# Which states' B-row multiplies VectorE takes in a token scan: state 12 in place of state 4

## The reference

```python
def scan_step(h, inputs):
    x_t, dt_t, B_t, C_t = inputs
    A_bar = jnp.exp(dt_t[..., None] * A)
    B_bar = dt_t[..., None] * B_t[:, None, :]
    h_new = A_bar * h + B_bar * x_t[..., None]
    y_t = (h_new * C_t[:, None, :]).sum(axis=-1)
    return (h_new, y_t)
```

## Time and profile before

| what | value |
|---|---|
| median of 3 runs | 335.23 us (334.68 to 344.01) |
| the profiled execution's own time | 334.67 us |
| its span | 332.9 us |
| busy, TensorE | 274.3 us (82%) |
| busy, VectorE | 264.8 us (80%) |
| busy, GpSimd | 256.7 us (77%) |
| busy, ScalarE | 191.6 us (58%) |

### The profile page before, as it was taken

How to read it: one execution, slowest core, us unless ns; L and a number is a source line. 1 busy time by engine, 2 the same in 40 slices (tenths; PEclk the granted TensorE clock), 3 DMA queues, 4 the chain that set the end, 5 groups by cost and what they waited for, 6 DMA issues and landing times. The chain is left out here.

```text
span 332.9 us, 4726 instructions
## 1 busy us (share of the span) xinstructions
PE 274.3 (82%) x1454; PEld 156.9 (47%) x1454; DVE 264.8 (80%) x289; ACT 191.6 (58%) x300; POOL 256.7 (77%) x134
## 2 busy tenths in 40 slices
PE   7899918875778589999889789997695787997996
PEld 4423402333435244346564243464564656765674
DVE  3465687998768898998798989998898887999711
ACT  2103931326895433478967354689738686888253
POOL 0009037999999998998999989999998689999500
PEclk9999976999798879999999899999969799999999
DMA  7980297587779999767699997676999999998301
GB/s 234 410 318 0 50 335 293 185 261 248 254 269 265 316 295 398 257 239 278 209 318 289 321 345 269 232 248 228 312 275 318 344 275 342 324 340 297 97 0 32
DMA packets 46889, 85.88 MB, mean 258 GB/s; under 512 B 7697, under 2 KB 24593, under 8 KB 46609
## 3 DMA queue, kind: packets, MB, share of 16 engines
q1 hardware_dynamic: 46464, 84.42, 76.5%
q10 hardware_dynamic: 400, 1.17, 1.3%
HBM read 75.62 MB, written 1.57 MB: 232 GB/s over the span
## 5 line engine op out<-in xcount | busy, mean ns | idle before, releaser
L1254 POOL TENSOR_TENSOR hc<-h,c_row 128x1024 f32<-128x1024 f32 (+1 forms) x79 | 154.4, 1963 | 16.9 <-DVE h L1383 13.8
L1243 POOL TENSOR_TENSOR ub<-u,b_row 128x1024 f32<-128x1024 f32 (+1 forms) x47 | 95.6, 2034 | 15.7 <-DMA b_row<-bc_dram 14.9
L951 ACT ACTIVATE decay<-delta,neg_a 128x512 f32<-128x512 f32 (+1 forms) x62 | 49.9, 815 | 65.4 <-DVE h L1383 65.2
L684 PEld LDWEIGHTS acc_y<-pack,hc 128*128 128x128 f32 x512 | 61.3, 149 | 47.9 <-issue 27.5
L684 PE MATMUL acc_y<-pack,hc 128*128 128x128 f32 x512 | 75.7, 289 | 9.9 <-POOL hc L1254 6.2
L1383 DVE TENSOR_TENSOR_SCAN h<-decay,ub 128x512 f32<-128x512 f32 (+1 forms) x40 | 64.9, 1621 | 15.4 <-POOL ub L1243 10.7
L626 PE MATMUL work<-q,kT 64*128 64x512 f32 x112 | 34.9, 702 | 17.8 <-DVE mixed L1409 13.5
L1409 DVE TENSOR_TENSOR mixed<-gam,work 128x512 f32<-128x512 f32 x56 | 35.6, 676 | 7.3 <-PE work L626 6.6
L978 ACT ACTIVATE decay<-u 128x512 f32<-128x512 f32 (+1 forms) x44 | 27.8, 639 | 20.7 <-DVE h L1383 20.4
L637 PE MATMUL acc_r<-mixed,v_sb 128*64 128x512 f32 x128 | 37.0, 658 | 1.1 <-DVE mixed L1409 1.0
L1383 DVE TENSOR_TENSOR_SCAN h<-decay_own,decay 128x512 f32<-128x512 f32 (+1 forms) x24 | 35.7, 1487 | 1.2
(11 more groups left out here) (226 smaller groups left out, 353.4 us busy)
## 6 DMA issues: line engine op xcount, KB each, us to landing
b_row<-bc_dram SPq DMA_DIRECT2D x64, 512.0 KB, 5.3
c_row<-bc_dram SPq DMA_DIRECT2D x64, 512.0 KB, 5.4
group_w<-expert_w SPq DMA_DIRECT2D x48, 128.0 KB, 4.7
gam<-gammaT SPq DMA_DIRECT2D x8, 512.0 KB, 10.4
expert_w<-routed_w SPq DMA_DIRECT2D x1, 2048.0 KB, 18.4
gam<-expert_w SPq DMA_DIRECT2D x16, 128.0 KB, 5.2
x_in<-xT SPq DMA_DIRECT2D x4, 256.0 KB, 9.2
pack<-packed ACTq DMA_DIRECT2D x1, 788.0 KB, 7.4
```

The source lines that it names most:

```text
L684: mm = nc.tensor.matmul(acc_y[:, to:to + P], hc[:, at:at + P], ident, start=(job.state == 0 and c % 4 == 0), stop=(job.state == STATES - 1 ...
L951: op = nc.scalar.activation(target, delta[:, job.image % 2, columns], ACT.Exp, scale=neg_a[:, job.state:job.state + 1])
L1243: nc.gpsimd.tensor_tensor(ub[:, ring(made, job.halves)], u[:, job.image % 2, tokens(q)], b_row[:, ring(job.at, job.halves)], ALU.mult).the ...
L1254: nc.gpsimd.tensor_tensor(hc[:, here], h[:, here], c_row[:, here], ALU.mult).then_inc(hc_ready, job.halves)
```

## The change

In images one to three VectorE drives states 0, 8, 10, 12 and 14, where it drove 0, 4, 8, 10 and 14. The last image is as before.

```diff
 VECTOR_JOBS = [q for q, job in enumerate(JOBS)
-               if job.state in ((0, 4, 8, 10, 14) if job.image not in SPLIT else (0, 2, 4, 5, 7, 9, 11, 13, 15))]
+               if job.state in ((0, 8, 10, 12, 14) if job.image not in SPLIT else (0, 2, 4, 5, 7, 9, 11, 13, 15))]
```

## The result

The changed kernel takes 345.92 us (median of 4 runs, 344.30 to 348.12), the kernel before 334.96; the ratio is 1.034, with a 95% interval of 1.029 to 1.039. The direction was right and the size was not: 341.7 us was forecast, with a range up to 344. The profiled execution of the changed kernel took 348.12 us (span 346.3), the longest of its four: 13.4 us over the span of 332.9 before, where the median shows 11.

What follows compares the result with a forecast made beforehand. GpSimd and VectorE, both nearly full, were taken to bound the kernel together, neither alone. Delays of 2.35, 3.15 and 1.55 us in images one to three make 7.05, taking 334.67 to 341.7 us; range 339.5 to 344.

Steps and rivals of the forecast that it cites:

- GpSimd's row without a pause: First half of images one to three: GpSimd's unbroken states 1 to 7 delay state 7's scan, 2.9 us in all.
- the waits of s5 to s7 for ub: Sign, first half: scans of states 5, 6 and 7 would each wait for GpSimd's ub; no size given.
- ScalarE's decay_own in front of V12: Second half: ScalarE's extra decay delays VectorE's state 12 multiply; 1.75 us each in images two and three.
- V12 waits: Sign at state 12: VectorE's multiply would wait about 1.6 us for ScalarE's copy.
- In image one 0.65 was forecast: Second half, image one: state 13's scan 0.65 us late, since an existing 0.80 us wait for GpSimd goes.
- TensorE's order is unchanged and the W that it waits for come with the scans.: TensorE, images one to three: its queue keeps its order and its W inputs follow the scans; costed at nothing.
- Of what follows in VectorE's queue nothing has waited, so the delay stays.: VectorE behind state 12, image two: following work had no waits to absorb the 1.75 us delay.
- State 14 is late as well: Rival: state 14's copy also comes late in each image, adding 5.2 us, 346.9 us; chance 0.06.
- The last image: Sign: the last image's length, from its first scan on, would be unchanged.
- By occupancy nothing changes.: Whole kernel: equal busy sums and GpSimd's same occupancy would leave 334.7 us; rival's chance 0.07.

Runs made afterwards that it cites:

- e1: Half the change against the kernel before: state 4 goes to GpSimd, state 12 stays there; 340.92 us, ratio 1.013.
- e9: The changed kernel itself, run again beside the kernel before on another chip; 346.53 us, ratio 1.039.
- e10: The changed kernel plus spare matmuls in TensorE's pauses in all three images; 342.56 us, ratio 1.026.
- e11: Control: the kernel before plus nine spare matmuls on TensorE in image two; 335.25 us, ratio 1.0035.
- e2: Other half alone against the kernel before: VectorE drives state 12 as well as 0, 4, 8, 10, 14; 343.55 us, ratio 1.029.
- e4: The change made in image two alone, images one and three as in the kernel before; 341.60 us, ratio 1.023.
- e5: The changed kernel with ScalarE's softplus parts moved behind the two copies of u for state 12; 341.71 us, ratio 1.020.
- e6: Against the kernel before: VectorE drives 0, 4, 8, 10, 12, 14, with decay_own made early in two buffers; 339.55 us, ratio 1.013.
- e7: The changed kernel with decay_own made early, in two buffers; 344.60 us, ratio 1.029.
- e8: The kernel before with decay_own made early, in two buffers; 334.62 us, ratio 0.997.

## Why the prediction was wrong, point by point

- *GpSimd's row without a pause, 2.9 us.* The mechanism is right: s7 begins 20.9 us behind U3 in images one and two of every profile of the change, with the waits of s5 to s7 for ub that were named. What it costs goes by U3's start, which the sum took from one profile. s7 of image two was 1.79 us late in e1, where U3 began 10.57 us behind s0, and 0.56 us late in e9, where its B row had landed in time and it began at 9.35 (before: 10.19). Image three was 0.20 us early in e1 and e9's 0.3 late. That e1's three numbers add up to 3.35, near 2.9, holds for that profile.
- *ScalarE's decay_own in front of V12, 1.75 us in images two and three.* The mechanism is right: 1.68 and 1.86 us more from s7 to s13 in e10, and V12 waits 1.56 us. In image one 0.65 was forecast; it was 0.88 in the changed kernel's profile and 1.75 in e10's. There s11 is 0.85 us later, and the clock was low for one long stretch before it (83.8 to 94.1) in place of two short ones (82.7 to 86.1 and 89.5 to 92.9 before); that the one makes the other I argue only.
- *"TensorE's order is unchanged and the W that it waits for come with the scans."* This step failed. It looked at TensorE's waits for W and not at those for f (L748) and for q (L563), which stand in line with s12. They were short before, 0.85 and 0.73 us, and grew to 1.73 and 1.59; behind them the clock fell, and 4.2 us were lost from s13 on in image two of the profiled execution (2.4 in e9's). Spare matmuls in the pauses brought the median back from 346.5 to 342.6 us. The engine was costed at nothing because its queue had not changed and it had idle time to spare; that idle time was what the clock was lost by.
- *"Of what follows in VectorE's queue nothing has waited, so the delay stays."* It stayed and grew: s15 and the next image's scores hang on TensorE through ScalarE's v_sb. At the full clock that chain had a slack of 0.80 us (ScalarE's wait behind v_sb, at 176.36 in the kernel before); at half the clock v_sb came 4.0 us later.
- *The rivals.* "State 14 is late as well", the only one on the slow side beyond the forecast, was the wrong place: copies for state 14 came in time (its V14 was not waiting in the changed profile). A fall of the granted clock was not among them, though the page before showed several (its row of granted clocks has tenths of 6 to 8 in nine of its forty slices, most of them where one image passes into the next), and the earlier trace rows have means of 0.95 and 0.93.
- *The last image* was as long as before to 0.3 us, as said. In other profiles it is shorter, 80.3 us in e9 and 79.3 in e11, where the last image has no spare matmuls either, so this agreement can't carry much.
- *By occupancy nothing changes.* The busy times did stay, on GpSimd, VectorE and ScalarE, and the time rose by 3.4%. The Trainium skill (Perfetto Trace Analysis, Identifying the Most-Contended Engine) goes by the engine with the highest occupancy. Read as a forecast it would have left the time where it was, and for this change of order the measurement decides against that reading.

## What to carry to other kernels

Where two engines hand work to each other and are both nearly full, the place of the pauses counts and not their sum: write out the slower one's queue through the longest row without a pause and add it up. Then follow the delay to every engine that waits for the late instruction, those with time to spare too. An idle TensorE that got about a microsecond more to wait here came back at half its clock, and that cost 2.0 to 5.2 us in image two, several times the delay; in one profile that can be read off a group of matmuls whose duration has doubled, and tested with spare matmuls in the pause.

## What the runs showed that I had not expected

- The granted clock fell to 0.50 around s13 of image two in each profile without spare matmuls in which q or L1448's f came about a microsecond later (pauses in front of L563 and L748 of 1.59 and 1.73 us in the change and in e9, 1.60 and 1.73 in e2, 1.59 and 1.72 in e4, 2.02 and 0.55 in e5, 0.55 and 1.72 in e6 and e7), and not there in those with 0.73 and 0.82 to 0.85 (before, e1). No single pause can be named as the cause: in e2, e4, e7 and e9 the low clock begins inside the pause in front of L748, 0.2 to 1.3 us after its start, and in the change, e5 and e6 up to 0.5 us behind its end. The sum of the pauses does not tell it either: in e8 the clock was low from 166.7 to 170.1 in image two, in which TensorE had paused for 1.23 us in front of its first layer-2 group and for no more than half a microsecond before q and f.
- What a fall costs went by how long it lasted. From s13 to the next s0 image two needs 13.98 us before. It needed 2.0 to 2.6 us more where the clock was low for about 7 us (e4, e5, e7, e9), 4.25 more where it was low for about 10 (the change, e6) and 5.15 more where it was low for about 14 (e2). In e8 the low stretch was over before s13 and cost nothing there. Groups of sixteen matmuls took 3.3 to 3.5 us in place of 1.90. That the two levels are 1.2 and 2.4 GHz is what the Trainium skill says (TensorE: Matmul & The Clock Gate, Part 1: The HAM clock gate); the trace shows the granted share fall from 1.00 to 0.50 and a group's time grow by a factor of 1.85 at most (3.52 to 1.90 us).
- It depends on what hangs on it, too. In images one and three of the changed kernel's profile the clock was low for as long as in image two or longer, and from s13 on they were no longer than before. In e9 and e10 image three lost 0.55 and 0.9 us there.
- It stays open what sets how long the clock stays low, and with it why single executions differ: the changed kernel's lie between 343.7 and 348.1 us, and only two of them have a profile here.
